# A grouped convolution inside a two-layer FFN kernel: direct form for the first two tiles, four-product form from the third, and unread products in TensorE's first idle stretches

## What is computed

```python
x = x + _L0_ffn_ref(_L0_cond_ref(x, ...), ...)      # per-batch mix of 8 kernels, then a sign-weight FFN
x = x + _L1_ffn_ref(_L1_cond_ref(x, ...), ...)      # grouped convolution, then an FFN with 8 LoRA experts

def _L1_cond_ref(x, c, weight, c_weight, bias):     # GROUPS = 4, K = 9, PAD = 4, 64 channels, L = 1024
    out = lax.conv_general_dilated(x, weight, window_strides=(1,), padding=[(4, 4)],
                                   dimension_numbers=('NCH', 'OIH', 'NCH'), feature_group_count=4)
    return out + jnp.einsum('nd,od->no', c, c_weight)[:, :, None] + bias[None, :, None]
```

## Time and profile before

| | us |
|---|---|
| median of 3 runs | 549.06 |
| lowest, highest | 548.24, 549.08 |
| profiled execution | 548.2 |
| its span, first to last instruction | 546.4 |
| PE busy | 524.1 |
| DVE busy | 312.3 |
| POOL busy | 254.9 |
| ACT busy | 121.3 |

### The profile page before, as it was taken

One profiled execution on the slowest core, in us unless ns is written; L12 is line 12 of the kernel. 1 busy time (PEld: TensorE's weight loads), 2 busy tenths in 40 slices (PEclk: granted clock), 3 DMA queues, 4 the chain that ended last, 5 costly groups with the idle time before them and its releaser, 6 DMA issues.

```text
span 546.4 us, 14325 instructions
## 1 busy us (share of the span) xinstructions
PE 524.1 (96%) x5717; PEld 446.5 (82%) x5717; DVE 312.3 (57%) x488; ACT 121.3 (22%) x289; POOL 254.9 (47%) x121
## 2 busy tenths in 40 slices
PE   5897999999999889899999999999999999999997
PEld 4675877887887778788988989889889898898896
DVE  4479998797776796345253374463543633634411
ACT  5633433434434231011011011010110110101100
POOL 0038767757747295661552642633615516336100
PEclk9999999999999899999999999999999999999999
DMA  8794455555578326514414244143142241341111
GB/s 314 245 382 171 161 202 189 190 187 207 196 220 239 102 90 186 158 43 121 122 47 151 96 62 150 54 112 126 62 130 101 57 156 70 91 136 62 40 40 38
DMA packets 57209, 75.21 MB, mean 138 GB/s; under 512 B 6432, under 2 KB 43488, under 8 KB 57184
## 3 DMA queue, kind: packets, MB, share of 16 engines
q1 hardware_dynamic: 56960, 74.48, 42.9%
q10 hardware_dynamic: 224, 0.36, 0.3%
HBM read 58.03 MB, written 16.79 MB: 137 GB/s over the span
## 4 chain that ended last, share of the span: by engine, by line
PE 86%; issue 4%; DVE 4%; POOL 3%; ACT 1%; DMA 0%; SPq 0%; DVEq 0%; POOLq 0%; ACTq 0%
PE bank L595 49%; PE bank L502 19%; PE bank L576 6%; PE bank L634 4%; PE bank L436 4%; PE bank L449 2%; PE bank L478 1%; POOL work L1100 1%; DVE parts L923 1%; POOL work L1093 1%; DVE mixes L988 1%; ACT parts L736 1%; DVE y_t L916 0%; DMA cst<-in_consts 0%; DVE y_t L894 0%
## 5 line engine op out<-in xcount | busy, mean ns | idle before, releaser
L595 PE MATMUL bank<-early,parts 128*128 128x320 f32 (+1 forms) x1152 | 207.2, 337 | 4.2 <-POOL mixes L1156 2.3
L595 PEld LDWEIGHTS bank<-early,parts 128*128 128x128 f32 x1152 | 184.6, 188 | 21.4 <-POOL mixes L1156 2.6
L502 PE MATMUL bank<-late,parts 128*128 128x512 f32 x512 | 129.8, 404 | 5.2 <-ACT parts L736 3.4
L502 PEld LDWEIGHTS bank<-late,parts 128*128 128x128 f32 x512 | 93.6, 191 | 26.6 <-ACT parts L736 4.0
L1152 POOL TENSOR_TENSOR xs<-raw 128x1024 f32<-128x1024 f32 x14 | 27.1, 1937 | 156.7 <-DMA raw_turned<-x_scratch 156.7
L595 PE MATMUL bank<-late,parts 128*128 128x512 f32 x384 | 94.1, 394 | 0.0
L923 DVE TENSOR_TENSOR parts<-y_t,parts 128x512 fp32r<-128x512 f32 x64 | 90.4, 1433 | 2.0 <-ACT parts L736 0.6
L595 PEld LDWEIGHTS bank<-late,parts 128*128 128x128 f32 x384 | 70.9, 188 | 16.0
L1100 POOL TENSOR_TENSOR work<-work 128x512 f32<-128x512 f32 x32 | 46.2, 1446 | 49.3 <-DVE work L931 48.2
L1051 DVE TENSOR_TENSOR qk<-bank,qk 128x256 f32<-128x256 f32 x16 | 6.8, 424 | 103.1 <-ACT qk L821 103.1
L736 ACT ACTIVATE parts<-y_t 128x512 fp32r<-128x512 f32 x64 | 39.5, 630 | 91.0 <-DVE y_t L980 49.4
(11 more groups left out here) (107 smaller groups left out, 472.7 us busy)
## 6 DMA issues: line engine op xcount, KB each, us to landing
xs<-in_x SPq DMA_DIRECT2D x16, 512.0 KB, 3.3
work<-in_x SPq DMA_DIRECT2D x16, 512.0 KB, 3.2
x_scratch<-work SPq DMA_DIRECT2D x16, 512.0 KB, 3.0
raw<-x_scratch SPq DMA_DIRECT2D x128, 64.0 KB, 2.8
raw_turned<-x_scratch SPq DMA_DIRECT2D x128, 64.0 KB, 2.5
work<-x_scratch SPq DMA_DIRECT2D x16, 512.0 KB, 3.6
out_tokens<-work SPq DMA_DIRECT2D x15, 512.0 KB, 2.7
stage<-in_wearly SPq DMA_DIRECT2D x8, 576.0 KB, 3.9
```

The source lines that it names most:

```text
L502: last = mm(bank[4 + h][:, :], parts[:, p, a, c, :], signs[:, c, h * HALF:(h + 1) * HALF], start=(k % 16 == 0), stop=(k % 16 == 15))
L595: return mm(dst, parts[:, p, a, c, :], w(b, c), start=(k == 0), stop=(close and k == 23))
```

## The change

Tiles 0 and 1 get a direct convolution. `product_conv` now multiplies `raw` itself with a full Toeplitz band (`band`, [128, 8, 128]): for each of eight blocks two steps of 128 columns and two of 64 that accumulate, so 64 products again. `add_context` becomes two additions per half of the tokens. The old form stays under the names `product_filter`, `add_filter` and `filter_inputs`, is used from tile 2 on, and reads its taps from a tile `taps`, made of a further input `tapin` that is loaded into `raw_turned[:, 1]`. The turned loads of tiles 0 and 1 and DVE's inputs for them go. SP loads `raw` and `raw_turned` of tile 2 as soon as tile 0's z is made, ahead of the bias, the last stores of x1 and the first residuals. POOL makes tile 2's inputs ahead of the first bias addition of stage two. And `keep_busy` issues products into `bank[4]` that nobody reads: one of 512 columns before the first real product, on a tile that DVE has cleared, and one of 256 and one of 128 after the small MLP.

```diff
-        band = sb("band", [P, 4, GROUPS, S])
+        band = sb("band", [P, 2 * GROUPS, P])
...
+        taps = sb("taps", [P, 2, GROUPS, S])
...
+        tap_src = raw_turned[:, 1, :, :].rearrange("p n q -> p (n q)")
+        tap_block = [tap_src[:, j * GROUPS * S:(j + 1) * GROUPS * S].rearrange("p (g n) -> p g n", g=GROUPS) for j in range(4)]
...
-            sp.dma_start(band[:, :, :, :].rearrange("p a g n -> p (a g n)"), toep).then_inc(band_loaded, 16)
+            sp.dma_start(band[:, :, :].rearrange("p a n -> p (a n)"), toep).then_inc(band_loaded, 16)
+            sp.dma_start(tap_src, tapin).then_inc(taps_loaded, 16)
...
-            load_raw(0, 0, False)
+            load_raw(0, 0)
             replace_x1(late_i, 0)
             next_chunk(late_i)
-            load_raw(0, 0, True)
             replace_x1(late_i, 1)
...
             sp.dma_start(xs[:, 0, :], late_pairs[3]).then_inc(late_loaded[3], 16)
-            load_raw(0, 1, False)
...
-            load_raw(0, 1, True)
+            load_raw(0, 1)
 
             replace_x1(last - 1, 1)
+            sp.wait_ge(z_biased, 2)
+            load_raw(1, 0)
+            load_raw(1, 0, True)
             sp.wait_ge(xb_ready, 2 * TILES)
...
+            def replace_out(i, p, first=False):
+                both = 4 * i + 2 * p + 2
+
+                sp.wait_ge(z_biased, both)
+                if not first:
+                    load_raw(i + 1, p)
+                    load_raw(i + 1, p, True)
+                load_row(ctx_row, i + 1, p, ctx_loaded)
+                store_out(i, p, both)
+                sp.wait_ge(out_stored[p], 16 * (i + 1))
+                load_resid(i + 1, p)
+
+            replace_out(0, 0, True)
+            replace_out(0, 1)
...
+            def keep_busy(operand, *columns):
+
+                for n in columns:
+                    mm(bank[4][:, 0:n], operand[:, 0:P], operand[:, 0:n], start=True, stop=True)
+
+            pe.wait_ge(idle_operand_cleared, 1)
+            keep_busy(weighted[:, :, :].rearrange("p s k -> p (s k)"), HALF)
             pe.wait_ge(consts_loaded[0], 16)
...
+            keep_busy(cst, 2 * P, P)
             pe.wait_ge(consts_loaded[2], 16)
...
-                pe.wait_ge(conv_in_ready, 6 * i + 3 * p + 3)
-
-            def product_conv(other):
+                pe.wait_ge(raw_loaded[p], (i + 1) * (16 * L8))
+
+            def product_conv(p, other):
+
+                low, high = slice(0, S), slice(S, P)
+                steps = ((low, 1, slice(0, P)), (high, 0, slice(0, P)), (low, 0, low), (high, 1, high))
+                for n in range(NBG):
+                    for k, (rows, s, cols) in enumerate(steps):
+                        into = (bank[n // 4], bank[other + n // 4])[k % 2]
+                        at = (n % 4) * P
+                        for g in range(2):
+                            last = mm(into[g * S:(g + 1) * S, at + cols.start:at + cols.stop],
+                                      raw[rows, p, n, s + g * S:s + (g + 1) * S],
+                                      band[rows, s * GROUPS + n % 4, cols], start=(k < 2), stop=(k >= 2))
+                        if n % 4 == 3 and k >= 2:
+                            last.then_inc(conv_done, 1)
+
+
+            def inputs_of_filter(i, p):
+
+                pe.wait_ge(conv_in_ready, 6 * i + 3 * p - 3)
...
-                    pe.wait_ge(band_made, 5)
+                    pe.wait_ge(band_loaded, 16)
+                    pe.wait_ge(pads_zeroed, 2)
                     pe.wait_ge(u_ready, 2 * TILES)
                     inputs_of_conv(0, 0)
-                    product_conv(2)
+                    product_conv(0, 2)
...
-                            inputs_of_conv(ni, q)
                             if late_ready:
+                                inputs_of_conv(ni, q)
 
                                 pe.wait_ge(out_scale_ready, 2 * TILES)
                             else:
+                                inputs_of_filter(ni, q)
...
-                    product_conv(4 + 2 * q)
+                    if late_ready:
+                        product_conv(q, 4 + 2 * q)
+                    else:
+                        product_filter(4 + 2 * q)
...
+            v.memset(weighted[:, :, :], 0.0).then_inc(idle_operand_cleared, 1)
...
-                if conv:
-                    dve.wait_ge(raw_loaded[0], 32 * L8)
-                    dve.wait_ge(pads_zeroed, 2)
-                    dve.wait_ge(y_done, 2 * TILES)
-                    conv_inputs(0)
...
+            v.tensor_copy(taps[:, 0], tap_block[0]).then_inc(taps_made, 1)
+            v.tensor_tensor(taps[:, 1], tap_block[1], tap_block[3], ALU.add).then_inc(taps_made, 1)
+            dve.wait_ge(taps_made, 2)
+            v.tensor_tensor(taps[low, 1], taps[low, 1], tap_block[2][low], ALU.add).then_inc(taps_made, 1)
+            v.tensor_tensor(taps[high, 1], taps[high, 1], tap_block[2][high], ALU.subtract).then_inc(taps_made, 1)
+            dve.wait_ge(taps_made, 4)
+            v.tensor_scalar(taps[:, 1], taps[:, 1], 0.5, None, ALU.mult).then_inc(taps_made, 1)
...
+            def add_context(i, p, other, halves=(0, 1)):
+
+                dve.wait_ge(ctx_loaded[p], 16 * (i + 1))
+
+                dve.wait_ge(z_lo, 4 * i + 2 * p)
+                by_group = lambda made: made[:, :].rearrange("p (n l c) -> p n l c", n=4, l=L8)
+                for h in halves:
+                    zt = z_t[:, :, 64 * h:64 * h + 64].rearrange("p l (n c) -> p n l c", c=CG)
+                    add = row_bc[:, p:p + 1, 64 * h:64 * h + 64].rearrange("p l (n c) -> p n l c", c=CG)
+                    dve.wait_ge(conv_done, 8 * i + 4 * p + 2 * h + 1)
+                    v.tensor_tensor(zt, by_group(bank[h]), add.broadcast_to([P, 4, L8, CG]),
+                                    ALU.add).then_inc(conv_halved, 1)
+                    dve.wait_ge(conv_done, 8 * i + 4 * p + 2 * h + 2)
+                    dve.wait_ge(conv_halved, 4 * i + 2 * p + h + 1)
+                    v.tensor_tensor(zt, by_group(bank[other + h]), zt, ALU.add).then_inc(z_biased, 1)
...
-            dve.wait_ge(raw_loaded[1], 32 * L8)
-            conv_inputs(1)
...
+                if first:
+                    add_context(ni, q, 4 + 2 * q, (0,))
+                elif ni is not None:
+                    add_filter(ni, q, 4 + 2 * q)
...
+                if ni is not None and not first:
+                    take_rest(ni, q, z_t, z_hi, z_lo, by_block)
+                elif first:
+                    take_rest(ni, q, z_t, z_hi, z_lo, by_token, (0,))
+                    add_context(ni, q, 4 + 2 * q, (1,))
+                    take_rest(ni, q, z_t, z_hi, z_lo, by_token, (1,))
...
+            def filter_inputs(i, p, first=False):
+
+                if not first:
+                    pool.wait_ge(conv_done, 4 * i + 2 * p + 4)
+                pool.wait_ge(raw_loaded[p], i * (32 * L8) + 16 * L8)
...
+            filter_inputs(1, 0, True)
+            add_bias1(0, 0)
+            add_bias1(0, 1)
+            filter_inputs(1, 1)
+            with pool.Fori(1, PAIRS - 1) as i:
                 for p in range(2):
                     add_bias1(i, p)
-                    conv_inputs(i + 1, p)
+                    filter_inputs(i + 1, p)
```

More of the change, by code:

```diff
@@ L61, with adaln_ffn_kernel @@
 R_HALF, R_TILE, R_END = 136, 264, 392
-def adaln_ffn_kernel(nc, x, consts, rows, mix, wsign, scales, bias0, toep, wearly, wlate, bm, bias1, out):
+def adaln_ffn_kernel(nc, x, consts, rows, mix, wsign, scales, bias0, toep, tapin, wearly, wlate, bm, bias1, out):
     x1_dram = nc.dram_tensor("x1_scratch", (TILES * P, H), F32, kind="Internal").ap()
@@ L313, in _, with load_raw @@
             late_i, last = PAIRS - 3, PAIRS - 1
-            def load_raw(i, p, turned):
+            def load_raw(i, p, turned=False):
                 sp.wait_ge(x1_stored[p], 16 * (i + 1))
@@ L576, in product_conv @@
                                 last = mm(into[a][r][g * S:(g + 1) * S, n * S:(n + 1) * S],
-                                          src[rows, n, g * S:(g + 1) * S], band[rows, a, n % 4, :], start=True, stop=True)
+                                          src[rows, n, g * S:(g + 1) * S], taps[rows, a, n % 4, :], start=True, stop=True)
                             if n == NBG - 1 and a == 1:
@@ L963, in _, with period0 @@
             mix_kernels(2, 0)
[L965 to L990 removed]
+            def period0(i, p, before, one, two=None, three=None, four=None):
                 scale_out(*before, 1)
@@ new lines, in add_filter @@
+            def add_filter(i, p, other):
+                dve.wait_ge(ctx_loaded[p], 16 * (i + 1))
+                dve.wait_ge(z_lo, 4 * i + 2 * p)
+                dve.wait_ge(conv_done, 4 * i + 2 * p + 6)
+                by_group = lambda made: made[:, :].rearrange("p (n l c) -> p n l c", n=NBG, l=4)
+                first, second = (z_t[:, 4 * h:4 * h + 4, :].rearrange("p l (n c) -> p n l c", c=CG) for h in range(2))
```

(18 more changed lines are left out.)

84 lines of the change are left out of this document (24 added, 60 removed).

## The result

The changed kernel takes 541.61 us (median of 4 runs, 541.31 to 542.80) against 549.07 for the kernel before (median of 4, 548.24 to 552.66): ratio 0.9856, 95% interval 0.981 to 0.9902. The profiled execution took 541.6 us with a span of 539.8; against the profile of before that is 6.6 us less.

A forecast was written before the change was run, and what follows sets the result against it. PE, busy 96% of the span, was taken as the bound. The middle's -5.63 and the start's +0.34 sum to -5.29 us: 542.9 from the profiled execution, 543.8 from the median, so 543.3 us, range 540.3 to 546.2.

The forecast's parts named there:

- First stall: PE's wait before 181.82, ahead of stage one's last tile, goes as DVE's inputs go: -1.95 us.
- the second: PE's stall before 200.33 goes, as tile 1's direct product needs only `raw`: -1.86 us.
- idle time of the row: Each of PE's three stalls at the change of stages priced at its bracketed idle time: 1.95, 1.86, 2.29 us.
- First convolution: Tile 0's convolution takes 3.03 us at full clock instead of 3.57: -0.54 us.
- Second convolution: Tile 1's convolution in direct form takes 3.03 us instead of 2.02: +1.01 us.
- The price of 3.03: Length of each direct convolution in us: the filter's 2.02 times 1.5 for its columns.
- Third stall: PE's wait before 224.65 for POOL's third-tile inputs goes with earlier loads and inputs: -2.29 us.
- Rival B: POOL's last weight split makes PE wait before its LoRA stretch: up to 2.8 us, time 546.1; chance 0.14.
- Rival C: Direct products in the convolutions do not overlap: 12.1 us each, time 561; chance 0.03.
- The start: Unread products ahead of the first y delay PE by +0.34 us (bounds 0 and 0.55).
- Rival A: Unread products at the start raise the clock early: 2.0 us gained, no delay, time 541.0; chance 0.28.

The follow-up runs named there:

- e5: The changed kernel with tile 2's sixteen loads and POOL's inputs for it back at their old places: 542.31 us.
- e8: The kernel before with two unread products of 512 columns in each of the three stalls at the change of stages: 548.48 us.
- e4: The kernel before with two unread products of 512 columns in the stall ahead of stage one's last tile: 550.3 us.
- e6: The kernel before with only tile 2's loads and POOL's inputs for it moved early, convolutions in the old form: 546.07 us.
- e2: The changed kernel with more unread products, in every gap of TensorE up to the first y: 544.05 us.
- e9: The changed kernel without unread products, DVE's block on the taps cut in three and put behind three late tiles of stage one: 540.45 us.
- e7: The changed kernel without unread products, DVE's whole block on the taps moved behind the last weight split: 544.14 us.
- e3: The changed kernel with 256 and 384 unread columns just ahead of the first FFN products in place of its own unread products: 542.19 us.
- e10: e9 with e3's unread products of 256 and 384 columns ahead of the first FFN products: 540.27 us.

## Why the prediction was right, point by point

**First stall: right, -2.24 for -1.95.** It went, and it cost more than its idle time. The same shows at the second (-2.13 for -1.86) and the third (-2.57 for -2.29). The 48 products of stage two's first two blocks run from start to next start in 197.47 - 190.35 = 7.12 us without a break; with the stall in them they took 202.29 - 193.04 = 9.25, so 2.13 went for a wait that its row gives as 1.86. The term "idle time of the row" was undersized by 0.27 to 0.29 each, 0.84 together. A row's idle time begins at the end of the last product, which in a dense run lies beyond the start of the next one, and the next one starts with nothing in flight; that reading of the rows was not tested by itself. But the surplus hardly depends on the length of the wait: in e5 a wait of 0.26 us cost 7.65 - 7.12 = 0.53, 0.27 more.

**First convolution: right in kind.** At a clock of 1.00 it took 2.84, so -0.73 for -0.54. **Second convolution:** +0.82 for +1.01. The price of 3.03 was 0.19 too high twice: 512 more columns, counted for the full array, cost 0.82 us, less than the filter's whole time scaled by columns. That the idle stretch, not the convolution, made the clock fall is shown by e8, with e4: with the stalls filled and the same convolutions the mean clock was 1.000 in 9 of 12 executions, without in 1 of 25.

**Third stall: right that it goes, wrong as to what it takes.** The prediction gave it to the early loads. e5 takes them away again and keeps all but 0.26 us of the gain: z of tile 0 comes 4.5 us earlier (189.43 + 0.68 = 190.1 before, 184.91 + 0.69 = 185.6 after), and everything on SP and POOL follows it. e6 shows the other way round that the early loads alone would have done it. The sum had it nearly right because the stall goes in either case.

**Rival B: did not decide.** POOL's last split ended at 202.19, 3.8 us ahead of PE's 205.96; POOL's operations were shorter too (2.66 and about 2.4 for 3.40 and 3.37), as DVE's inputs are gone. **Rival C: no.** The direct products overlap.

**The start: right for the profile, open for the time.** The first y product came 0.40 late (forecast 0.34), and 0.32 of it reached 176. Rival A did not occur: the y products stayed at 1.98 and 1.99 us, and with more unread products in e2 too. (By the earlier trace rows the two y products lose 1.8 us at half speed, where the prediction has 1.9; nothing hangs on it.) But the loss is measured against a start in which the constants had landed at 2.68. In the executions profiled without unread products the first real product started between 2.68 and 3.21 and the first y between 9.95 and 10.46 (10.58 in e8); in the three profiled with the change's unread products at 3.33 and 10.36 or 10.37. On the whole time no loss is shown.

**The size, and some luck.** The measured 541.6 lies nearer to rival A's 541.0 than to the forecast's 543.3, though A did not occur: by the time alone the wrong rival would seem to have won, and only the timelines tell them apart. Steps of -6.57 for the forecast -5.29: 0.84 from the restarts, 0.38 from the two convolutions, the rest small. The medians differ by 7.5, more than the two profiles. That fits with the kernel before losing further time to its clock in most executions (its profile had one fall, at a mean of 0.997, and 39 of the 63 executions had a lower mean), though the clocks of the four behind this median are not all known. The prediction treated the clock as one loss of 0.5 us in the first convolution. It is a risk at a stall, seen in these profiles behind the first, the second and the one at 54 us, and the change removes three of the four longest stalls.

## What to carry to other kernels

Price a stall of TensorE, where it bounds the kernel, at its idle time plus what the restart costs, here about 0.28 us, and add the clock: round an idle stretch of 1.65 us or more it fell here in some executions and not in others, so look at the spread of the times together with the mean clock before trusting a single profile. Where two causes fall together, the loads of an edit may look needed and not be: undo them singly. Before moving work into DVE's idle time, look at what POOL does there; here small pieces in tiles with slack (e9) were better than a block in a gap (e7).

## What the hardware showed that was not expected

The granted clock fell to 0.50 round idle stretches of 1.65 to 3.06 us, and not round others of the same length, in the same execution too: in the profile of before behind the 1.95 but not the 1.86 and 2.29 us, in e4 behind the 1.88, in e6 behind the 1.70 at 53.78 and the 2.11 but not the 1.81, in e7 in the last 0.5 us of the 3.06, in the changed kernel's second profile behind the 1.65, 1.8 us after PE had gone on. The time of the kernel before goes with its mean clock: 7.7 us between 1.000 and 0.988 or less.

Full speed at the start, read from the lengths of the products (the clock column reads 1.00 there all along), came between about 24.4 and 27.7 us in all profiles but two, whatever stood ahead of the first y, even with PE dense from 1.5 us on (e2). In e3 it came at 18.5, and with the same edit in e10 just ahead of 24.2. Nor is it fixed for one kernel: the changed kernel's two profiles have it at 26.6 and 24.4. What decides it stays open.
